# A 32-row strip per head for the score operands, and a group's products in runs

## The reference

```python
xn = _layernorm(x)
q, k, v = (xn @ w.T + b for ...)                   # 16 heads, Dh = 8
scores = einsum('bthd,bshd->bhts', q, k) * Dh ** -0.5
scores = where(x[:, :, 0] != 0, scores, -inf)      # mask on the keys
attn = softmax(scores) @ v @ wo.T + bo             # per head
# experts: top 2 of 8 by xn @ gate_w, capacity int(1.25 * n * 2 / 8) = 1280
out = x + attn + sum over the two experts of weight * (gelu(xn @ c_fc + fc_bias) @ c_proj + proj_bias)
```

## Time and profile before

| | |
|---|---|
| runs | 804.57 and 805.71 us, median 805.14 |
| span of the profiled execution, first to last instruction | 651.9 us |
| around the span (median less span) | 153.2 us |
| PE busy | 602.8 us (92%) |
| DVE busy | 473.7 us (73%) |
| ACT busy | 397.7 us (61%) |
| POOL busy | 226.3 us (35%) |
| mean granted clock of TensorE | 0.975 |

### The profile page before, as it was taken

One profiled execution on the slowest core, in us unless ns is written; L12 is line 12 of the kernel. 1 busy time (PEld: TensorE's weight loads), 2 busy tenths in 40 slices (PEclk: granted clock), 3 DMA queues, 4 the chain that ended last, 5 costly groups with the idle time before them and its releaser, 6 DMA issues.

```text
span 651.9 us, 12725 instructions
## 1 busy us (share of the span) xinstructions
PE 602.8 (92%) x3474; PEld 378.7 (58%) x3474; DVE 473.7 (73%) x904; ACT 397.7 (61%) x782; POOL 226.3 (35%) x218
## 2 busy tenths in 40 slices
PE   2775999899999999999999999999999999999971
PEld 1542455455555558965579755599555797555421
DVE  6889988988888893179852488821889416988856
ACT  2662376667768667457784377754776844776770
POOL 9765512877773030000110000300003002777775
PEclk9997799999999999999999999999999999999995
DMA  3776246224222161112521122411225111642141
GB/s 87 247 252 201 77 174 199 68 65 121 89 86 81 50 151 42 41 55 77 148 53 40 40 69 74 109 40 40 74 69 148 41 40 50 121 112 61 49 131 48
DMA packets 59543, 60.62 MB, mean 93 GB/s; under 512 B 9541, under 2 KB 44357, under 8 KB 59514
## 3 DMA queue, kind: packets, MB, share of 16 engines
q1 hardware_dynamic: 53722, 46.49, 25.5%
q0 software_dynamic: 5792, 13.79, 7.1%
HBM read 33.87 MB, written 25.18 MB: 91 GB/s over the span
## 4 chain that ended last, share of the span: by engine, by line
PE 68%; DVE 12%; POOL 9%; issue 6%; DMA 2%; SPq 1%; ACT 1%; DVEq 0%; POOLq 0%; ACTq 0%
PE bD L945 15%; PE bPV L982 14%; PE bA L969 13%; PE bD L1075 11%; POOL hid L552 5%; POOL xn_all L552 4%; DVE nmax L770 4%; PE bA L1063 3%; PE bA L1067 3%; PE bA L1064 3%; PE bD L991 2%; PE bA L953 2%; DVE xe L709 1%; PE bD L1004 1%; DVE acc L841 1%
## 5 line engine op out<-in xcount | busy, mean ns | idle before, releaser
L770 DVE TENSOR_REDUCE nmax<-bD 128x1 f32<-128x512 f32 x512 | 338.6, 687 | 37.0 <-PE bD L945 35.5
L628 ACT ACTIVATE probs<-bA 128x512 f32<-128x512 f32 x512 | 263.0, 600 | 74.9 <-PE bA L969 73.3
L945 PE MATMUL bD<-K,Q 128*128 128x512 f32 x512 | 202.5, 438 | 4.7 <-DVE nmax L770 2.5
L969 PE MATMUL bA<-Q,K 128*128 128x512 f32 x512 | 159.7, 394 | 0.4 <-ACT probs L628 0.4
L945 PEld LDWEIGHTS bD<-K,Q 128*128 128x128 f32 x512 | 97.0, 192 | 105.5 <-DVE nmax L770 87.2
L982 PE MATMUL bPV<-probs,v_aug 128*32 128x512 f32 x1024 | 136.4, 605 | 0.5 <-ACT probs L628 0.5
L969 PEld LDWEIGHTS bA<-Q,K 128*128 128x128 f32 x512 | 95.9, 188 | 22.4 <-ACT probs L628 4.8
L542 POOL TENSOR_TENSOR wfc_hi<-wfc,ones 128x512 fp32r<-128x512 f32 x8 | 10.3, 1285 | 280.5 <-DMA pjb<-in_pjb 280.5
L1075 PE MATMUL bD<-wpj,hid 128*128 128x128 f32 x640 | 73.4, 275 | 0.0
L1075 PEld LDWEIGHTS bD<-wpj,hid 128*128 128x128 f32 x640 | 72.4, 192 | 0.0
L820 DVE TENSOR_TENSOR ye<-bD,pjb 128x512 f32<-128x512 f32 (+1 forms) x24 | 14.5, 603 | 79.5 <-PE bD L1075 79.5
(11 more groups left out here) (105 smaller groups left out, 475.0 us busy)
## 6 DMA issues: line engine op xcount, KB each, us to landing
slot_x<-hid POOLq DMA_DIRECT2D x10, 512.0 KB, 3.2
xe<-slot_x SPq DMA_DIRECT2D x8, 640.0 KB, 4.6
slot_y<-ye SPq DMA_DIRECT2D x8, 640.0 KB, 3.7
q_parts<-hid SPq DMA_DIRECT2D x8, 512.0 KB
k_parts<-hid SPq DMA_DIRECT2D x8, 512.0 KB
Q<-q_parts SPq DMA_DIRECT2D x32, 128.0 KB
K<-k_parts SPq DMA_DIRECT2D x64, 64.0 KB
Q<-q_parts SPq DMA_DIRECT2D x64, 64.0 KB
```

The source lines that it names most:

```text
L628: nc.scalar.activation(probs[:, (g % 2) * 4 + h, :], bA[h][:], ACT.Exp, scale=SCALE).then_inc(s_exp, 1)
L770: nc.vector.tensor_reduce(nmax[q][:, k, head:head + 1], bank()[:], AX.X, ALU.max, negate=True).then_inc(s_dd, 1)
L945: done(nc.tensor.matmul(free()[:], Q[u][:, s // 2, k * P:(k + 1) * P], K[u][:, s, :], start=True, stop=True))
L969: nc.tensor.matmul(bA[h][:], K[u][:, 4 * q + h, j * P:(j + 1) * P], Q[u][:, 2 * q + h // 2, :], start=True, stop=True).then_inc(s_st, 1)
```

## The change

The operands of a head now lie in one strip of 32 partitions: four heads of a quad in four strips of `K` and `Q`, which become [128, 2, 512] (quad, token). A strip has 24 rows of parts (q: hi, hi, lo; k: hi, lo, hi), the mask row, and two rows for the maximum's parts. Rows 0 to 24 are used for the maximum, rows 0 to 26 for the transposed scores. The DRAM tensors `q_rows` and `k_rows` have this form, so that a quad is loaded by two DMAs; a batch is written by seven DMAs where it was three, the constant rows are written to DRAM at the start by four DMAs of POOL, and the maxima go into Q by four DMAs where it was two. The four products of a reduction step are now of the four heads and one block of 128 queries, where it was four blocks of one head.

```diff
-ROWS = 4 * DH
-TAIL = 2 * ROWS
-MASKROW = TAIL + 4
+QUAD = 4
+STRIP = P // QUAD
+ROW_MASK = 3 * DH
+ROW_MAX = ROW_MASK + 1
+NR_MAX, NR_EXP = ROW_MASK + 1, ROW_MASK + 3
+HI, LO = 0, 1
+Q_ROWS, K_ROWS = (HI, HI, LO), (HI, LO, HI)
-WR_DMAS, LOAD_DMAS = 3, 11
-ZERO_DMAS, ROW_DMAS = 10, 6
+WR_DMAS, LOAD_DMAS, MAX_DMAS = 7, 2, 4
+ZERO_DMAS, ROW_DMAS = 10, 4
 ...
-                sp.dma_start(q_parts[b], parts[0, q]).then_inc(s_wr[q], 16)
-                sp.dma_start(k_parts[b], parts[1, q]).then_inc(s_wr[q], 16)
+                for w, stack, order in ((0, q_rows, Q_ROWS), (1, k_rows, K_ROWS)):
+                    for r, part in enumerate(order):
+                        sp.dma_start(stack[b, :, r * DH:(r + 1) * DH, :], parts[w, q][:, part, :]).then_inc(s_wr[q], 16)
 ...
+                h0 = u * UH + QUAD * q
+                for tile, stack in ((Q[u], q_rows), (K[u], k_rows)):
+                    sp.dma_start(tile[:, q, :].bitcast(F32), stack[b, h0:h0 + QUAD].rearrange("h r t -> (h r) t")
                                  ).then_inc(s_load[u][q], 16)
 ...
-                for pair in range(2):
-                    sp.dma_start(Q[u][TAIL:TAIL + 4, 2 * q + pair, :].bitcast(F32),
-                                 nmT[q][4 * pair:4 * pair + 4, :].bitcast(F32)).then_inc(s_nq[q], 16)
+                for h in range(QUAD):
+                    at = STRIP * h + ROW_MAX
+                    sp.dma_start(Q[u][at:at + 2, q, :].bitcast(F32), nmT[q][2 * h:2 * h + 2, :].bitcast(F32)
+                                 ).then_inc(s_nq[q], 16)
 ...
-            for t in (K[0], K[1], Q[0], Q[1], zeros4):
-                nc.gpsimd.memset(t[:].bitcast(F32), 0.0).then_inc(s_fill, 1)
-            pool.wait_ge(s_fill, 5)
+            pool.dma_start(row_ones, tail_d[4:5, 0, :].to_broadcast([P, T])).then_inc(s_ones, 16)
+            nc.gpsimd.memset(row_zeros, 0.0).then_inc(s_fill, 1)
+            pool.wait_ge(s_fill, 1)
+            pool.wait_ge(s_ones, 16)
+            every_q, every_k = (t.rearrange("b h r t -> (b h) r t") for t in (q_rows, k_rows))
+            for stack, r0, r1, src in ((every_q, ROW_MASK, ROW_MAX, row_ones), (every_q, ROW_MAX, STRIP, row_zeros),
+                                       (every_k, ROW_MAX, NR_EXP, row_ones), (every_k, NR_EXP, STRIP, row_zeros)):
+                pool.dma_start(stack[:, r0:r1, :], src[:, None, :].to_broadcast([P, r1 - r0, T])).then_inc(s_rows, 16)
 ...
-                for k in range(first, first + n):
-                    done(nc.tensor.matmul(free()[:], Q[u][:, s // 2, k * P:(k + 1) * P], K[u][:, s, :], start=True, stop=True))
+                for h in range(first, first + n):
+                    done(nc.tensor.matmul(free()[:], strip(Q[u], q, h, NR_MAX, slice(k * P, (k + 1) * P)),
+                                          strip(K[u], q, h, NR_MAX), start=True, stop=True))
 ...
-                    nc.tensor.matmul(bA[h][:], K[u][:, 4 * q + h, j * P:(j + 1) * P], Q[u][:, 2 * q + h // 2, :],
-                                     start=True, stop=True).then_inc(s_st, 1)
+                    nc.tensor.matmul(bA[h][:], strip(K[u], q, h, NR_EXP, slice(j * P, (j + 1) * P)),
+                                     strip(Q[u], q, h, NR_EXP), start=True, stop=True).then_inc(s_st, 1)
 ...
-                ahead(0, 2)
+                ahead(0, 3)
                 if g >= 2:
                     with_v(b, g - 2)
 ...
                 if new_maxima:
                     maxima(b * HALVES + g // 4 + 1, (g // 4 + 1) % 2, b * GB + g)
-                ahead(2, 1)
-                scores(b, g, 0, 2, new_maxima, last)
+                scores(b, g, 0, 4, new_maxima, last)
                 ahead(3, 1)
-                scores(b, g, 2, 2, new_maxima, last)
```

More of the change, by code:

```diff
@@ L137, in build @@
         v_all = sb("v_all", [P, NT, C])
-        K = [sb(f"K{u}", [P, UH, T], F32R) for u in range(UNITS)]
-        Q = [sb(f"Q{u}", [P, UH // 2, T], F32R) for u in range(UNITS)]
-        zeros4 = sb("zeros4", [4, 2, T], F32R)
+        K = [sb(f"K{u}", [P, 2, T], F32R) for u in range(UNITS)]
+        Q = [sb(f"Q{u}", [P, 2, T], F32R) for u in range(UNITS)]
         probs = sb("probs", [P, 8, T])
@@ L201, in build @@
         s_fill = sem("s_fill")
+        s_ones = sem("s_ones")
         s_rows = sem("s_rows")
@@ L352, in load_quad @@
-                sp.dma_start(qd[0:ROWS], qs[:, pair0:pair0 + 2, :]).then_inc(s_load[u][q], 16)
-                for e in range(2):
-                    sp.dma_start(kd[e * 2 * DH:(e + 1) * 2 * DH, e, :, :], ks[e, :, pair0:pair0 + 2, :]
-                                 ).then_inc(s_load[u][q], 16)
[L357 to L362, removed]
@@ L457, in _ @@
             nc.gpsimd.tensor_copy(prefix_r[:], prefix[:]).then_inc(s_prefix, 1)
[L459 to L464, removed]
             def front(b, q):
@@ L522, in _ @@
             nc.gpsimd.memset(hid_f[:, 0:per], 0.0).then_inc(s_fill, 1)
-            pool.wait_ge(s_fill, 9)
-            pool.wait_ge(s_nq[0], 32)
+            pool.wait_ge(s_fill, 5)
+            pool.wait_ge(s_nq[0], MAX_DMAS * 16)
             for h in range(ZERO_DMAS):
@@ L609, in maxima @@
                 act.wait_ge(s_nt, m + 1)
-                wait(act, s_nq[q], k * 32)
+                wait(act, s_nq[q], k * (MAX_DMAS * 16))
                 nc.scalar.copy(nmT[q][:], bA[0][0:8, :]).then_inc(s_ne, 1)
@@ L765, in scores_max @@
             def scores_max(s):
-                q, head = (s // 4) % 2, s % 4
-                for k in range(TT):
+                q, k = (s // TT) % 2, s % TT
+                for head in range(QUAD):
                     take()
@@ L772, in scores_max @@
                     d.step()
-                if head == 3:
+                if k == TT - 1:
                     dve.wait_ge(s_dd, d.value())
@@ L937, in done, with strip @@
                 d.step()
+            def strip(tile, q, h, rows_used, cols=slice(0, T)):
+                return tile[STRIP * h:STRIP * h + rows_used, q, cols]
             def scores_for_max(b, u, s, first, n):
-                q = s // 4
-                if s % 4 == 0 and first == 0:
+                q, k = s // TT, s % TT
+                if k == 0 and first == 0:
                     pe.wait_ge(s_load[u][q], b * (LOAD_DMAS * 16) + LOAD_DMAS * 16)
-                for k in range(first, first + n):
-                    done(nc.tensor.matmul(free()[:], Q[u][:, s // 2, k * P:(k + 1) * P], K[u][:, s, :], start=True, stop=True))
+                for h in range(first, first + n):
+                    done(nc.tensor.matmul(free()[:], strip(Q[u], q, h, NR_MAX, slice(k * P, (k + 1) * P)),
+                                          strip(K[u], q, h, NR_MAX), start=True, stop=True))
             def maxima(m, q, n=None):
```

29 lines of the change are left out of this document (9 added, 20 removed).

## The result

The changed kernel takes 1002.8 us (two runs, 995.5 and 1010.1) against 805.1: 1.246 times the kernel before (95% interval 1.236 to 1.256), 198 us slower. The forecast of 823 us and its range of 783 to 862 miss it; of the directions it gave slower the most weight (0.52). Where the runs of one kernel lie more than 1.5% apart, ratios here go by the shorter ones, and all times are given.

The account below looks back on a forecast made before the run. The prediction took PE to be full before and a loop through DVE's fourth reduction to bind after the change: 805.1 + 17.1 (turns) - 0.4 (start) + 1.2 (maxima DMAs) = 823 us, range 783 to 862.

Parts of the forecast that it names:

- rival 4: PE's clock stays at 1.2 GHz as it waits for DVE each group: 898 us, 967 if throughout; chance 0.11.
- Plain loop 2.94: Plain attention group: the links from one fourth reduction's end to the next sum to 2.94 us, against 3.04 before.
- 0.43 from third product to values: Link in the plain group on PE: from the third product's weight load to the values' load, 0.43 us.
- DVE as the releaser: Plain group: the third product waits for its bank until DVE's fourth reduction ends, then loads 0.03 us later.
- Strips side by side, 0.02: Plain group: the four transposed scores overlap on four strips and add 0.02 us to the loop.
- Maxima groups 4.04: Groups that turn maxima, four a turn: the fourth product stands behind ACT's copy, loop 4.04 us against 3.38 before.
- Turn 55.2: A turn of 16 groups takes 55.2 us, 2.8 more than 52.43; times 6.1 turns gives +17 us.
- Rival 3: Strips don't overlap at all: plain loop 3.61 us, a turn 10.9 longer, whole 877 to 894, taken as 880; chance 0.06.
- The start, -0.4: Before the first products: zero fills saved up to 4 us, against 1.6 for batch writes and 2 for constant rows.
- 153.2 us around the span, unchanged: Median less the profiled 651.9 us span is 153.2 us, left unchanged in the forecast.
- the reasoning on the end: The 28 groups after the last expert lie beside POOL's gathers and cost nothing until some 10 us later.

Follow-up runs that it names:

- e4: The changed kernel with all four heads' score products in strip 0, so few rows and no overlap (other heads' scores not computed): 1127.9 us.
- e3: The changed kernel with every score product over all 128 rows and the exponential's scale set to 0: 896.6 us (890.2 and 903.1).
- e1: The changed kernel's strips with the group's order of the kernel before: 812.5 us, ratio 1.011 to the kernel before.
- e14: Strips in the order of the kernel before, with at most two indirect transfers under way: four runs, 723.1 to 752.4 us, ratio 0.906 to the kernel before.
- e5: The kernel before, unchanged, profiled again: 803.4 us in the median; the profiled run took 805.1 with a span of 803.2.
- e2: The kernel before, operands of 128 rows, with only the new order (three products, values, four scores, one product): 887.6 us, ratio 1.105.
- e9: The changed kernel plus two zero-weight products over 128 rows in most groups, ahead of the third product for the maximum: 906.3 and 921.0 us.
- e6: The changed kernel plus three zero-weight products over 128 rows per group, ahead of the wait for the exponentials: 977.5 us, ratio 1.216 to the kernel before.
- e7: Strips in the order of the kernel before, plus two zero-weight products over 128 rows per group: 855.3 us, ratio 1.067 to the kernel before.
- e12: The changed kernel with its 128 indirect transfers replaced by direct ones of the same size: 865.1 us (859.9 and 870.2).
- e11: The kernel before, with POOL waiting for each indirect transfer to land before issuing the next: 879.2 us, ratio 1.096.
- e13: The kernel before, with at most two of POOL's indirect transfers under way: 700.1 us, ratio 0.871.
- e8: The kernel before, with its 128 indirect transfers replaced by direct ones of the same size, to and from fixed places: 645.6 us, ratio 0.803.

## Why the prediction was wrong

**The step that failed: the clock** (rival 4, given 0.11). The forecast charged every link at 2.4 GHz; the attention ran at 1.2. Rival 4 had the place and nearly the price (plain loop 2.94 + 1.48 = 4.42, measured 4.59; turn 79, measured 84.4; the whole 967 if it held throughout) but went by two wrong reasons. I tied it to PE's waiting, and set against it a stretch of the front with waits that kept 2.4 GHz. That stretch has products over all rows. e4 (no waiting, few rows, 1.2 GHz) and e3 (waiting, all rows, 2.4 GHz) show that the rows are what sets the two apart. The Trainium skill (TensorE: Matmul & The Clock Gate, Part 1: The HAM clock gate) says that the clock follows how busy PE has recently been. Busy time in the trace is not that: e4's 20.00 of 20 us came with a clock of 0.50.

Rows are not all of it. With strips and the old order (e1, e14) the clock is at 1.2 GHz in some stretches and at 2.4 in others; with strips and the new order it is at 1.2 in nearly all; with full rows it is at 2.4 in either order, stalls apart (e5, e2). So for four strips side by side the order's wait and the few rows act together. By what measure the clock goes stays open.

**The split.** The normalisations of the changed kernel against those of e5: to the first one +25.2 us, through the first stall +4.0, the next four half turns +57.5, the four batches with experts +82.0 (from 263.35 to 345.36), the half turn with the second stall +5.9, the rest +30.4. Together that is the whole difference of the two spans, 205 us. At 2.4 GHz, by e9's turns of 58.0 against 52.5, some +34 over 6.1 turns would be there, and with the +10 of the front about 850 us in all. So about 34 us are the order's and 10 the front's; the other 150 or so are the clock's. This last division is worked out, since no run had strips, new order, no fillers and 2.4 GHz throughout.

**Step by step.**
- Plain loop 2.94: right (2.95), and so was each link: 0.43 from third product to values, DVE as the releaser.
- Strips side by side, 0.02: nearly. From the first score to the fourth product it is 576.32 - 575.99 = 0.33, where the sum had 0.25. The Trainium skill (TensorE: Matmul & The Clock Gate, section Measured speedup vs the span model) with its 3.07 for four row strips gave an estimated 0.30; the trace is nearer to that. It doesn't show in the loop.
- Maxima groups 4.04: right (4.07 in e9). Turn 55.2: 2.8 low (58.0 in e9, which has fillers).
- Rival 3 (no overlap, 3.61) fell, but its price was right for e2 (3.64). Its whole was added up wrongly at the low end: 10.9 a turn more than the forecast's 823 gives 889 and not 877.
- The start, -0.4: wrong by 10. The first reduction begins at 66.97, 56.95 in e5. I gave a batch 4.8 us, with 374 GB/s for a full DMA. It takes 6.7 (POOL's mask rows at 33.77, 40.53, 47.10), the DMA engines move 286 GB/s at 92% busy, and POOL waits 3.2 to 3.9 us in each batch for the write of the mask. The bytes were a little low too: 24 rows of q and 24 of k with the mask row, for 16 heads at 2 KB, are 1.61 MB and not 1.54.

```profile
33.77 1.91 POOL L456 TENSOR_SCALAR mrow<-ye 1x512 fp32r<-1x512 f32 x1
39.20 1.27 POOL L460 TENSOR_TENSOR v_all<-v_all,bv_s 128x512 f32 x1 [3.51 <-DMA k_rows<-mrow]
40.53 1.91 POOL L456 TENSOR_SCALAR mrow<-ye 1x512 fp32r<-1x512 f32 x1
```

  Whether bytes or the seven issues of SP bind it was not tried.
- "153.2 us around the span, unchanged": wrong as a reading, nearly right as a number. They are two stalls inside, and the two stretches that hold them grew by 9.9 us. But the reasoning on the end was built on it: that 28 groups lie beside POOL's gathers and cost nothing holds only for the execution without stalls. In a run with stalls POOL is done before the last turns, and the +30.4 at the end counts in full.

## What to carry to other kernels

Fewer rows per product can cost PE its clock: before splitting the array into strips, look for the granted clock of a stretch in which all products have few rows, and price every link of the loop at both levels. When a span and a time are far apart, find the missing time before leaving it alone; here it was 151 us, and a limit on the transfers got 103 of them back. Limit how many indirect transfers are under way, and start them early enough for the slower pace.

## What the runs showed of the hardware

- PE can be busy without a gap and be granted 1.2 GHz, when its products use few rows (e4: 25 to 27 rows of one strip, 199.59 of 200 us busy, clock 0.52). Zero-weight products over 128 rows bring 2.4 GHz back in most stretches (e6 and e7; e9 in part). Three of them take 0.90 us in e6's chain.
- Products on four row strips run together: four in 0.51 us, where four over all rows take 1.19 (e2, both at 2.4 GHz); at 1.2 GHz four take 0.80 (e12).
- Indirect transfers of 64 KB issued every 1.28 us without a limit left PE without a matmul for up to 24 us at a time, DVE with three or four instructions in 40 us and ACT with four to seven, at DMA shares of 0.13 and 0.21, so it is not bandwidth (e5). One at a time nothing is held (e11), with two under way a little (e13). As many direct transfers on the same queue hold nothing (e8). What the engines wait for in a stall the trace calls "another core or an unknown queue"; it stays open.
- The same kernel was profiled without these stalls once (span 651.9 us) and with them another time (803.2), while all its timed runs were at 800 to 807.
